# A window of three row transfers and two tiles on GpSimd's queue in place of bursts of four: a two-pass mixture-of-experts block with local attention

## The chip, the core and the metric

The kernel runs on one core of one Trainium2 chip. The metric is the device time of one execution in microseconds (us), as the median of several executions. Five engines work in parallel and wait for each other through semaphores: PE (matrix products), DVE (vector), ACT (activations), POOL (GpSimd) and SP (a queue that only issues transfers). Here POOL issues all indirect (scattering) transfers, and SP all others.

## The reference

The input is 32 sequences of 256 tokens with 128 channels. Half of a mixture-of-experts layer is added to it, then attention over the last 9 positions, then half of the same mixture-of-experts layer again:

```
x = x + 0.5 * ffn(layernorm(x))       # pass 1
x = x + attn(layernorm(x))
x = x + 0.5 * ffn(layernorm(x))       # pass 2

def ffn(xt):                          # 8192 tokens, 8 experts, 2 of them for each token
    probs, idx = top_k(softmax(xt @ Wg + bg), 2)
    h  = gelu(xt @ W1[e] + b1[e])     # 128 -> 512
    eo = h @ W2[e] + b2[e]            # 512 -> 128
    return probs[0] * eo[idx[0]] + probs[1] * eo[idx[1]]
```

Attention has 16 heads of 8 channels; each position sees itself and the 8 before it.

## The kernel before

The tokens lie in SBUF in 4 groups of 2048. Both passes go over the groups; the text counts the group scatters of both passes as q = 0 to 7 (q = 4 is group 0 in pass 2). For the experts the work is cut into seven parts: groups 0, 1, 2 and 3 of pass 1 are a part each (0 to 3), groups 0 and 1 of pass 2 are part 4 together, group 2 is part 5, group 3 is part 6.

For each group the router (DVE's `route`) works out a slot for each token and choice. ACT (`highs`) and DVE (`lows`) make the rows that are to be scattered, in four chunks of eight rows into the two halves of the buffer `hl`; a row is 128 tokens with 144 words each. POOL (`scatter_rows`, line 579) sends each row with one indirect transfer to the DRAM tensor `x_sorted` of its part, where it is sorted by expert. A chunk's half of `hl` is free for the chunk after next when all its rows have landed: ACT waits for that at line 669 before the cast at line 670. When all rows of a part have landed (`rows_sorted`, line 456) and the part's plan is ready, SP begins to load the part's tiles (`load_x`, lines 466 and 470): 256 or 128 slots of one expert, transposed, and their row numbers and gates, `tile_ids`.

PE multiplies a tile with W1 (line 949) and W2 (lines 960 and 966), with ACT's gelu between (line 756). DVE (`take_y`, line 1412) scales the result into `y_sb`, which has four places; it waits until the results of the tile four before have landed. POOL (`scatter_y`, line 596) scatters them to `y_pairs`, with two transfers for a wide tile of 256 slots and one for a narrow tile. SP loads the ids of a tile only when the results of the tile eight before have landed. When a part's results have all landed they are read back as `y_in` and added to x.

What each engine does in which order is fixed: five strings (`PE_ORDER`, `DVE_ORDER` and so on) say from which stream of work the engine issues its next step, and every engine issues strictly in that order. A step that waits holds up all that stands behind it on the same engine. On POOL the streams are the rows (`s`) and the tiles' results (`y`).

In pass 1 POOL issues a chunk's eight rows one after the other with no wait between. In pass 2 it issues four rows (`BURST`), then waits until all four have landed, before it takes its next step. Results of tiles are issued as soon as DVE has written them. `carry_waits` is one semaphore instruction, put ahead of a transfer to hold its waits.

Of the kernel before, what the change touches and what calls it, by code (L numbers as in the profile page):

```python
# [41 lines left out]
J = 16  # L42
# [9 lines left out]
Q = 4  # L52
JQ = J // Q
# [3 lines left out]
DMA = 16  # L57
SPLITS = (((0,), (1,), (2,), (3,)), ((0, 1), (2,), (3,)))
LOADS = 4
SUMMED_BY_DVE = (1, 3, 5, 7)  # L60
BURST = 4
B2_LO = 32
ROOT_START = 1597463007.0

# [95 lines left out]
def macaron(nc, x, Wq, Wk, Wv, Wo, Wg, bg, W1, b1, W2, b2, out):  # L160
    B, S, _ = x.shape
    N = B * S
    G = N // (P * J)
    PARTS = [gs for parts in SPLITS for gs in parts]
    PASS = [f for f, parts in enumerate(SPLITS) for _ in parts]
# [21 lines left out]
    def y_moves(ring, n):  # L187
        return DMA * sum(t.halves for t in ALL_TILES[:n] if t.ring == ring)
# [9 lines left out]
    with ExitStack() as ctx:  # L198
        def sb(name, shape, dt):
            return ctx.enter_context(nc.sbuf_tensor(name, shape, dt))  # L200

        def sem(name):
            return ctx.enter_context(nc.semaphore(name))

        def sems(name, n):
            return [sem(f"{name}{i}") for i in range(n)]
# [27 lines left out]
        hl = sb("hl", [P, 2, JQ, 2, ROW // 2], F32)  # L234
# [117 lines left out]
        hi_ready = sem("hi_ready")  # L352
        hl_ready = sem("hl_ready")
        slots_ready = sem("slots_ready")
        rows_scattered = sems("rows_scattered", 2)
        plan_ready = sem("plan_ready")
        ends_ready = sem("ends_ready")
        tails_cleared = sems("tails_cleared", NP)
# [23 lines left out]
        y_scattered = sems("y_scattered", 4)  # L382
# [5 lines left out]

        N_CONSTS = 9
        POOL_STEPS = 21 + NP  # L390
        SCATTERS = J * DMA

        def sums_before(g, c):

# [5 lines left out]
        def carry_waits(eng):  # L400
            eng.sem_inc(waits_carried)
# [29 lines left out]
        def _(sp):  # L431
# [24 lines left out]
            def rows_sorted(p):  # L456
                sp.wait_ge(tails_cleared[p], (1 + E) * DMA)
                sp.wait_ge(plan_ready, p + 1)
                for r in range(2):
                    sp.wait_ge(rows_scattered[r], (PASS[p] * G + PARTS[p][-1] + 1) * SCATTERS)  # L460

            def load_x(t):
                row = sp.value_load(tile_row[0:1, t.in_map:t.in_map + 1], min_val=0, max_val=SLOTS[t.p] - t.slots)
# [15 lines left out]
            def tiles():  # L479
                for t in ALL_TILES:  # L480
                    if t.at == 0:
                        clear_tails(t.p)
                        rows_sorted(t.p)
                    load_x(t)
                    yield
# [46 lines left out]
        def _(pool):  # L532
# [17 lines left out]
                               in_=window_mask[:].rearrange("p (j w) -> p j w", w=W), compare_op=ALU.is_ge,  # L550
# [3 lines left out]
                               in_=earlier[:].rearrange("o (e f) -> o e f", f=E), compare_op=ALU.is_gt,  # L554
# [16 lines left out]
            def scatter_rows(f, g):  # L571
                q, p = f * G + g, PART_OF[f * G + g]
                pool.wait_ge(slots_ready, q + 1)
                for c in range(Q):
                    pool.wait_ge(hl_ready, Q * q + c + 1)
                    carry_waits(pool)
                    for i in range(2 * JQ):
                        at = g * (J * 2) + c * (2 * JQ) + i
                        pool.indirect_dma_start(  # L579
                            out=x_sorted[p],  # L580
                            out_offset=bass.IndirectOffsetOnAxis(ap=slots_all[:, at:at + 1], axis=0),
                            in_=hl[:, c % 2, i // 2, i % 2, :], in_offset=None).then_inc(rows_scattered[c % 2], DMA)
                        if f and (i + 1) % BURST == 0:
                            pool.wait_ge(rows_scattered[c % 2], q * SCATTERS + (c // 2 * (2 * JQ) + i + 1) * DMA)
                            carry_waits(pool)
                            if i + 1 < 2 * JQ:
                                yield
                    yield

            def scatter_y():  # L590
                for t in ALL_TILES:
                    pool.wait_ge(ids_loaded[t.n % IDS], (t.n // IDS + 1) * DMA)
                    pool.wait_ge(y_ready, t.n + 1)
                    carry_waits(pool)
                    for i in range(t.halves):
                        pool.indirect_dma_start(  # L596
                            out=y_pairs, out_offset=bass.IndirectOffsetOnAxis(ap=tile_ids[:, t.n % IDS, i, 0:1].bitcast(U32), axis=0),
                            in_=y_sb[:, t.ring, i, :], in_offset=None, bounds_check=2 * N - 1, oob_is_err=False
                        ).then_inc(y_scattered[t.ring], DMA)
                    yield  # L600
# [10 lines left out]
        def _(act):  # L611
# [52 lines left out]
            def highs():  # L664
                for q in range(2 * G):
                    for c in range(Q):
                        act.wait_ge(norm_r.xn_ready, q * PAIRS + (c + 1) * (PAIRS // Q))
                        if q or c >= 2:
                            act.wait_ge(rows_scattered[c % 2], q * SCATTERS + c // 2 * (2 * JQ * DMA))
                        act.copy(hl16[:, c % 2, :, :, 0:D], xn_at[q][:, c * JQ:(c + 1) * JQ, :].rearrange("p j (o d) -> p j o d", o=1)  # L670
                                 .to_broadcast([P, JQ, 2, D])).then_inc(hi_ready, 1)
                        yield
# [769 lines left out]
```

## Time and profile before

| | |
|---|---|
| time of three executions | 1208.0, 1210.67 and 1205.4 us, median 1208.0 |
| span of the profiled execution, first to last instruction | 1193.9 us |
| PE busy | 919.0 us (77%) |
| POOL busy | 669.9 us (56%) |
| DVE busy | 644.4 us (54%) |
| ACT busy | 500.2 us (42%) |
| indirect transfers of rows | 256 |
| indirect transfers of results | 305 |

The profile is of one more execution, whose own time is not among the three; its span is 14.1 us below their median. "Busy" counts only execution, not waiting: an engine that is busy for less than the span waits for the rest, and what it waits for is read from the timelines and the chain below. In a timeline the brackets at the end of a row hold the idle time of the engine just before that instruction, and what ended it.

### The profile page before, as it was taken

How to read it: one execution, taken by the hardware profiler on the slowest of the kernel's cores; microseconds unless marked ns; L12 is line 12 of the kernel's file. 1: busy time of each engine (PE TensorE's matmuls, PEld its weight loads, DVE VectorE, ACT ScalarE, POOL GpSimd, SP SyncE). 2: the span in 40 equal slices, each digit the busy share in tenths (PEclk: the TensorE clock that was granted, in tenths of full speed). 3: DMA queues.
4: the chain of work that ended last, by engine and by line, in shares of the span. 5: the costliest groups of instructions: out<-in, count | busy, mean ns of one | idle time of the engine just before them, and what ended most of it. 6: DMA issues, size and time to landing. Idle time of an engine off the chain costs nothing.

```text
span 1193.9 us, 22506 instructions
## 1 busy us (share of the span) xinstructions
PE 919.0 (77%) x6345; PEld 762.5 (64%) x6345; DVE 644.4 (54%) x1309; ACT 500.2 (42%) x1215; POOL 669.9 (56%) x593
## 2 busy tenths in 40 slices
PE   3446868567897798988898838998988868865984
PEld 3334747456775587777777725677766756754874
DVE  6655133423147587898979998687851511110222
ACT  4433524334534273655644415634434433322432
POOL 2475445446387766455668556356765555555452
PEclk9999769889898799999999978989985988897997
DMA  8813212252113421026112121223222223432683
GB/s 274 235 55 73 55 44 50 65 137 67 42 58 62 134 54 41 19 59 139 33 39 55 23 96 55 45 52 68 50 60 53 51 59 84 116 97 69 154 190 120
DMA packets 170344, 96.44 MB, mean 81 GB/s; under 512 B 137696, under 2 KB 154390, under 8 KB 169332
## 3 DMA queue, kind: packets, MB, share of 16 engines
q1 hardware_dynamic: 152276, 59.29, 21.9%
q0 software_dynamic: 17952, 35.71, 9.5%
q8 instruction: 60, 0.98, 0.4%
q14 instruction: 56, 0.46, 0.1%
HBM read 25.77 MB, written 52.35 MB: 65 GB/s over the span
## 4 chain that ended last, share of the span: by engine, by line
PE 41%; issue 16%; DMA 10%; POOL 9%; another core or an unknown queue 8%; DVE 6%; SPq 6%; ACT 3%; ACTq 0%; POOLq 0%; DVEq 0%
PE bank L966 18%; PE bank L949 12%; POOL x_sorted L579 7%; DMA x_sorted<-hl,slots_all 5%; PE bank L854 3%; DMA x_sb<-in_L_attn_x 2%; PE bank L960 2%; ACT h_f L756 1%; POOL y_pairs L596 1%; SPq L476 1%; PE bank L840 1%; PE bank L867 1%; SPq L466 1%; SPq L452 1%
## 5 line engine op out<-in xcount | busy, mean ns | idle before, releaser
L596 POOL DMA_INDIRECT y_pairs<-y_sb,tile_ids x305 | 359.5, 1179 | 330.0 <-issue 215.9
L756 ACT ACTIVATE h_f<-bank,b_cols 128x256 f32<-128x256 f32 (+1 forms) x736 | 264.1, 439 | 443.3 <-PE bank L949 298.3
L579 POOL DMA_INDIRECT x_sorted<-hl,slots_all x256 | 301.9, 1179 | 179.4 <-issue 86.8
L966 PE MATMUL bank<-w_sb,h_f 128*128 x2440 | 355.2, 299 | 22.6 <-issue 15.3
L966 PEld LDWEIGHTS bank<-w_sb,h_f 128*128 128x128 f32 x2440 | 315.3, 206 | 45.1 <-issue 28.2
L949 PE MATMUL bank<-xsT,w_hl 128*128 128x256 f16 (+1 forms) x2208 | 263.3, 270 | 56.6 <-issue 20.9
L949 PEld LDWEIGHTS bank<-xsT,w_hl 128*128 x2208 | 201.2, 104 | 93.8 <-issue 66.7
L1412 DVE TENSOR_TENSOR y_sb<-bank,tile_ids 128x256 f32<-128x256 f32 (+1 forms) x184 | 68.8, 375 | 342.2 <-PE bank L966 169.0
L960 PE MATMUL bank<-b_hl,ones_b 64*128 x184 | 49.5, 269 | 72.8 <-DVE y_sb L1412 59.8
L960 PEld LDWEIGHTS bank<-b_hl,ones_b 64*128 64x128 f16 x184 | 17.1, 93 | 113.2 <-issue 110.6
L1197 DVE TENSOR_TENSOR prod<-score,qkv 128x2304 f32<-128x2304 f32 x32 | 81.6, 2550 | 0.2
L1151 DVE TENSOR_TENSOR prod<-qkv 128x2304 f32<-128x2304 f32 x32 | 81.4, 2551 | 0.2
L867 PE MATMUL bank<-prod,ident 128*128 128x256 f32 x288 | 67.3, 384 | 2.9 <-DVE prod L1197 2.5
L854 PE MATMUL bank<-prod,ident 128*128 128x288 f32 x256 | 65.4, 413 | 0.4 <-DVE prod L1151 0.4
L685 ACT COPY qkv<-bank 128x384 f32<-128x384 f32 (+1 forms) x96 | 41.3, 450 | 50.1 <-PE bank L840 22.2
L867 PEld LDWEIGHTS bank<-prod,ident 128*128 128x128 f32 x288 | 53.7, 192 | 10.7 <-DVE prod L1197 3.6
L854 PEld LDWEIGHTS bank<-prod,ident 128*128 128x128 f32 x256 | 49.1, 194 | 15.2 <-DVE prod L1151 1.5
L1035 DVE TENSOR_TENSOR hl<-xn_r,hl 128x1024 f16<-128x1024 f32 x24 | 29.3, 1223 | 43.3 <-ACT hl L670 33.9
L840 PE MATMUL bank<-wqkv,xnT_p 128*128 128x384 f32 x128 | 48.8, 509 | 3.5 <-ACT qkv L685 3.5
L670 ACT CAST hl<-xn_r 128x1024 f16<-128x1024 f32 x24 | 24.9, 1044 | 59.4 <-DMA x_sorted<-hl,slots_all 59.4
L614 ACT ACTIVATE xn_r<-x_sb,shift_r,rstd_r 128x128 f32<-128x128 f32 x96 | 39.0, 486 | 10.7 <-DVE shift_r L1022 10.7
L793 PE MATMUL bank<-wg_sb,xnT_p 128*128 128x8 f32 x128 | 27.8, 358 | 8.8 <-issue 5.6
(159 smaller groups left out, 851.3 us busy)
## 6 DMA issues: line engine op xcount, KB each, us to landing
y_in<-y_pairs SPq DMA_DIRECT2D x28, 512.0 KB
x_sorted<-no_rows SPq DMA_DIRECT2D x7, 720.0 KB
y_pairs<-y_sb,tile_ids POOLq DMA_INDIRECT x305
x_sb<-in_L_attn_x SPq DMA_DIRECT2D x4, 1024.0 KB, 5.7
x_sorted<-hl,slots_all POOLq DMA_INDIRECT x256
x_sorted<-no_rows SPq DMA_DIRECT2D x56, 72.0 KB
out<-x_sb SPq DMA_DIRECT2D x3, 1024.0 KB
xsT<-x_sorted SPq DMA_TRANSPOSE x184
```

The source lines that it names most:

```text
L579: pool.indirect_dma_start(out=x_sorted[p], out_offset=bass.IndirectOffsetOnAxis(ap=slots_all[:, at:at + 1], axis=0), in_=hl[:, c % 2, i // ...
L596: pool.indirect_dma_start(out=y_pairs, out_offset=bass.IndirectOffsetOnAxis(ap=tile_ids[:, t.n % IDS, i, 0:1].bitcast(U32), axis=0), in_=y ...
L756: ins = act.activation(h_part(t, b)[:, k, :], bank[h_banks.uses[u][0]][:, k * t.slots:(k + 1) * t.slots], ACT.Gelu, bias=b1_cols[:, bass.d ...
L840: pe.matmul(prep_bank[k % PREPS][:, 0:3 * D], xnT_p[:, k - RADIUS, 1:1 + P], wqkv[:], start=True, stop=True).then_inc(qkv_done, 1)
L854: ins = pe.matmul(score_bank[c % 2][:, 0:JH * W * HEADS].rearrange("p (n h) -> p n h", h=HEADS), ident[:], products[:, :, d, :], start=(d ...
L867: ins = pe.matmul(score_bank[c % 2][:, 0:JH * D].rearrange("p (j d) -> p j d", d=D), ident[:], prod[:, c % 2, :, w, :], start=(w == 0), st ...
L949: ins = pe.matmul(dst, w1_flat[:, bass.ds((e * HC + c) * (2 * P) + ws * P, P)], slots_of(t)[:, s], start=(n == 0), stop=(n == 2))
L960: pe.matmul(into, ones_b2[:], b2_hl[:, bass.ds(e * D, D)].rearrange("k (o d) -> k o d", o=1) .to_broadcast([2 * B2_LO, t.halves, D]), star ...
L966: ins = pe.matmul(into[:, half, :], h_part(t, c // t.per)[:, c % t.per, half * P:(half + 1) * P], w2_flat[:, bass.ds((e * HC + c) * D, D)] ...
L1151: ins = dve.tensor_tensor(prod[:, prod_of[c]], q_ap.to_broadcast([P, JH, W, D]), windows(lo, D), ALU.mult)
L1197: dve.tensor_tensor(prod[:, c % 2].rearrange("p j w (h d) -> p j w h d", d=DK), score[:, lo:lo + JH].rearrange("p j w (h o) -> p j w h o", ...
L1412: dve.tensor_tensor(y_sb[:, t.ring, 0:t.halves], y_bank(t), tile_ids[:, t.n % IDS, 0:t.halves, 1:2] .to_broadcast([P, t.halves, D]), ALU.m ...
```

## The change

The bursts of four are dropped. Rows are counted through both passes (`n`), and from the fourth on each waits, before it is issued, until the row three before it has landed; the semaphores of rows are four (`n % 4`) in place of two (one for each half of `hl`). So at most three rows are in flight, in both passes. Results of a tile wait until the results of the tile two before have landed. ACT and SP wait for the same rows as before, on four semaphores in place of one or two.

```
-BURST = 4
+WINDOW = 3
+ROW_RING = 4
...
-        rows_scattered = sems("rows_scattered", 2)
+        rows_scattered = sems("rows_scattered", ROW_RING)
...
-        SCATTERS = J * DMA
+        CHUNK = 2 * JQ // ROW_RING * DMA
...
-                for r in range(2):
-                    sp.wait_ge(rows_scattered[r], (PASS[p] * G + PARTS[p][-1] + 1) * SCATTERS)
+                for r in range(ROW_RING):
+                    sp.wait_ge(rows_scattered[r], (PASS[p] * G + PARTS[p][-1] + 1) * Q * CHUNK)
...
                     pool.wait_ge(hl_ready, Q * q + c + 1)
-                    carry_waits(pool)
                     for i in range(2 * JQ):
                         at = g * (J * 2) + c * (2 * JQ) + i
+                        n = (q * Q + c) * (2 * JQ) + i
+                        if n >= WINDOW:
+                            pool.wait_ge(rows_scattered[(n - WINDOW) % ROW_RING], ((n - WINDOW) // ROW_RING + 1) * DMA)
+                        carry_waits(pool)
                         pool.indirect_dma_start(
                             out=x_sorted[p],
                             out_offset=bass.IndirectOffsetOnAxis(ap=slots_all[:, at:at + 1], axis=0),
-                            in_=hl[:, c % 2, i // 2, i % 2, :], in_offset=None).then_inc(rows_scattered[c % 2], DMA)
-                        if f and (i + 1) % BURST == 0:
-                            pool.wait_ge(rows_scattered[c % 2], q * SCATTERS + (c // 2 * (2 * JQ) + i + 1) * DMA)
-                            carry_waits(pool)
-                            if i + 1 < 2 * JQ:
-                                yield
+                            in_=hl[:, c % 2, i // 2, i % 2, :], in_offset=None).then_inc(rows_scattered[n % ROW_RING], DMA)
+                        if f and i + 1 == JQ:
+                            yield
                     yield
...
                     pool.wait_ge(y_ready, t.n + 1)
+                    if t.n >= 2:
+                        pool.wait_ge(y_scattered[(t.n - 2) % 4], y_moves((t.n - 2) % 4, t.n - 1))
                     carry_waits(pool)
...
                         if q or c >= 2:
-                            act.wait_ge(rows_scattered[c % 2], q * SCATTERS + c // 2 * (2 * JQ * DMA))
+                            for r in range(ROW_RING):
+                                act.wait_ge(rows_scattered[r], (q * Q + c - 1) * CHUNK)
```

The order of the instructions stays the same on every engine; only waits differ. On POOL, at the start of pass 1, the first rows of part 0 stand so before (`x_sorted0` is that part's tensor, "x7" seven alike in a row):

```order
L579 DMA x_sorted0<-hl,slots_all 18688x144 [waits hl_ready,pool_step,slots_ready]
L579 DMA x_sorted0<-hl,slots_all 18688x144 x7
L579 DMA x_sorted0<-hl,slots_all 18688x144 [waits hl_ready]
L579 DMA x_sorted0<-hl,slots_all 18688x144 x7
L579 DMA x_sorted0<-hl,slots_all 18688x144 [waits hl_ready]
```

And so with the change (`rows_scattered0` to 3 are the four semaphores in turn):

```order
L583 DMA x_sorted0<-hl,slots_all 18688x144 [waits hl_ready,pool_step,slots_ready]
L583 DMA x_sorted0<-hl,slots_all 18688x144 x2
L583 DMA x_sorted0<-hl,slots_all 18688x144 [waits rows_scattered0]
L583 DMA x_sorted0<-hl,slots_all 18688x144 [waits rows_scattered1]
L583 DMA x_sorted0<-hl,slots_all 18688x144 [waits rows_scattered2]
L583 DMA x_sorted0<-hl,slots_all 18688x144 [waits rows_scattered3]
L583 DMA x_sorted0<-hl,slots_all 18688x144 [waits rows_scattered0]
L583 DMA x_sorted0<-hl,slots_all 18688x144 [waits hl_ready,rows_scattered1]
```

No row but the chunk's first had a wait; now every row from the fourth on waits for the one three before it.

On POOL, the end of part 5's results and the last rows of part 6 (`x_sorted6`; `ids_loaded` and `y_ready` belong to the results) stand so before:

```order
L596 DMA y_pairs<-y_sb,tile_ids 16384x128 [waits ids_loaded0,y_ready]
L596 DMA y_pairs<-y_sb,tile_ids 16384x128 [waits ids_loaded1,y_ready]
L579 DMA x_sorted6<-hl,slots_all 18688x144 x4
L579 DMA x_sorted6<-hl,slots_all 18688x144 [waits rows_scattered0,hl_ready]
L579 DMA x_sorted6<-hl,slots_all 18688x144 x3
L579 DMA x_sorted6<-hl,slots_all 18688x144 [waits rows_scattered1]
L579 DMA x_sorted6<-hl,slots_all 18688x144 x3
L596 DMA y_pairs<-y_sb,tile_ids 16384x128 [waits rows_scattered1,ids_loaded2,y_ready]
```

And so with the change:

```order
L599 DMA y_pairs<-y_sb,tile_ids 16384x128 [waits y_scattered2,ids_loaded0,y_ready]
L599 DMA y_pairs<-y_sb,tile_ids 16384x128 [waits y_scattered3,ids_loaded1,y_ready]
L583 DMA x_sorted6<-hl,slots_all 18688x144 [waits rows_scattered1]
L583 DMA x_sorted6<-hl,slots_all 18688x144 [waits rows_scattered2]
L583 DMA x_sorted6<-hl,slots_all 18688x144 [waits rows_scattered3]
L583 DMA x_sorted6<-hl,slots_all 18688x144 [waits rows_scattered0]
L583 DMA x_sorted6<-hl,slots_all 18688x144 [waits hl_ready,rows_scattered1]
L583 DMA x_sorted6<-hl,slots_all 18688x144 [waits rows_scattered2]
```

The waits between the bursts have become waits of each row for the third before it. The results behind the rows no longer wait for those rows (`rows_scattered1` in the last line of before), but, as the first two lines here, for the results of the tile two before.

## Rows read from the trace of the kernel before

**Rows 1.** The page's chain that ended last, by engine and line.
```profile
PE 41%; issue 16%; DMA 10%; POOL 9%; another core or an unknown queue 8%; DVE 6%; SPq 6%; ACT 3%; ACTq 0%; POOLq 0%; DVEq 0%
PE bank L966 18%; PE bank L949 12%; POOL x_sorted L579 7%; DMA x_sorted<-hl,slots_all 5%; PE bank L854 3%; DMA x_sb<-in_L_attn_x 2%; PE bank L960 2%; ACT h_f L756 1%; POOL y_pairs L596 1%; SPq L476 1%; PE bank L840 1%; PE bank L867 1%; SPq L466 1%; SPq L452 1%
```

**Rows 2.** Waits of POOL: who waited for whom, total us, times, longest.
```profile
POOL x_sorted L579 <- DMA x_sorted<-hl,slots_all: 48.4, 21, 4.1
...
POOL y_pairs L596 <- DMA x_sorted<-hl,slots_all: 15.9, 6, 3.5
```

**Rows 3.** POOL's timeline in pass 2: start, us, instruction, [idle before <-releaser].
```profile
620.18 0.99 POOL L596 DMA_INDIRECT y_pairs<-y_sb,tile_ids  x1 [2.49 <-DMA x_sorted<-hl,slots_all]
...
857.16 1.97 POOL L596 DMA_INDIRECT y_pairs<-y_sb,tile_ids  x1 [2.33 <-DMA x_sorted<-hl,slots_all]
...
1006.12 0.99 POOL L596 DMA_INDIRECT y_pairs<-y_sb,tile_ids  x1 [4.54 <-DVE y_sb L1412]
...
1059.23 0.99 POOL L596 DMA_INDIRECT y_pairs<-y_sb,tile_ids  x1 [3.51 <-DMA x_sorted<-hl,slots_all]
...
1077.04 0.95 POOL L579 DMA_INDIRECT x_sorted<-hl,slots_all  x1 [0.30 <-issue]
1080.22 0.96 POOL L579 DMA_INDIRECT x_sorted<-hl,slots_all  x1 [2.23 <-DMA x_sorted<-hl,slots_all]
...
1087.12 0.96 POOL L579 DMA_INDIRECT x_sorted<-hl,slots_all  x1 [2.15 <-DMA x_sorted<-hl,slots_all]
...
1094.17 0.99 POOL L596 DMA_INDIRECT y_pairs<-y_sb,tile_ids  x1 [2.31 <-DMA x_sorted<-hl,slots_all]
```

**Rows 4.** The chain in order of time, two stretches: start, us, what.
```profile
693.98 4.29 DMA x_sorted<-hl,slots_all
...
1077.04 2.29 DMA x_sorted<-hl,slots_all
1079.37 0.08 issue
1079.46 0.76 issue
```

**Rows 5.** POOL's timeline in pass 1, where rows and results alternate.
```profile
346.19 1.00 POOL L596 DMA_INDIRECT y_pairs<-y_sb,tile_ids  x1 [0.30 <-issue]
347.50 0.96 POOL L579 DMA_INDIRECT x_sorted<-hl,slots_all  x1 [0.30 <-issue]
```

**Rows 6.** POOL's timeline at the seventh row of all.
```profile
50.02 4.94 POOL L579 DMA_INDIRECT x_sorted<-hl,slots_all  x1 [0.30 <-issue]
```

**Rows 7.** POOL's transfers, 46 to 48 us: packets, MB, share of 16 engines.
```profile
q0 software_dynamic: 27, 0.05, 8.7%
```

**Rows 8.** DVE's timeline at seven places.
```profile
49.70 4.41 DVE L1292 SCALAR_TENSOR_TENSOR w_hl<-qkv,w_hl 128x4096 f16<-128x4096 f32 x1
...
623.87 0.42 DVE L1412 TENSOR_TENSOR y_sb<-bank,tile_ids 128x256 f32<-128x256 f32 x1 [4.31 <-issue]
...
725.10 1.22 DVE L1035 TENSOR_TENSOR hl<-xn_r,hl 128x1024 f16<-128x1024 f32 x1 [2.99 <-ACT hl L670]
...
743.96 0.19 DVE L1356 TENSOR_TENSOR tile_expert<-onehot 1x40 int32<-1x40 f32 x1
...
877.47 1.23 DVE L1035 TENSOR_TENSOR hl<-xn_r,hl 128x1024 f16<-128x1024 f32 x1 [2.93 <-ACT hl L670]
...
1011.86 0.42 DVE L1412 TENSOR_TENSOR y_sb<-bank,tile_ids 128x256 f32<-128x256 f32 x1 [1.64 <-remote]
...
1096.71 0.29 DVE L1412 TENSOR_TENSOR y_sb<-bank,tile_ids 128x128 f32<-128x128 f32 x1 [10.40 <-DMA y_pairs<-y_sb,tile_ids]
```

**Rows 9.** PE's timeline at the ends of the scatters of q = 4 and 5.
```profile
619.61 4.15 PE L854 MATMUL bank<-prod,ident 128*128 128x288 f32 x16 [0.39 <-DVE prod L1151]
...
762.45 1.93 PE L949 MATMUL bank<-xsT,w_hl 128*128 128x256 f16 x12 [2.75 <-DMA xsT<-x_sorted]
```

**Rows 10.** ACT's timeline at the last cast of q = 5.
```profile
724.02 1.04 ACT L670 CAST hl<-xn_r 128x1024 f16<-128x1024 f32 x1 [4.45 <-DMA x_sorted<-hl,slots_all]
```

## The prediction, made before the changed kernel ran

> **What bounds the kernel now.** I began with the chain of work that ended last. No engine fills it: PE holds 41%, and 5% are landings of rows (`DMA x_sorted<-hl,slots_all`) beside 7% of POOL issuing them [rows 1]. Landings stand on a chain only where somebody stands still until a transfer is down, so next I read POOL's waits: 27 waits on rows, 48.4 + 15.9 = 64.3 us in all [rows 2]. In pass 1 POOL has no such wait in the code; these are the drains behind the bursts of pass 2. POOL's timeline shows how one looks: after the fourth row of a burst the engine idles 2.23 us where it idles 0.30 us between two rows [rows 3]. The chain splits that wait: the row lands 2.29 us after its issue began, and POOL starts again 0.08 + 0.76 = 0.84 us later [rows 4]. Whether a drain costs the kernel anything must be read at each place, from what DVE, ACT and PE do at that moment: their orders are fixed, and work that reaches them earlier is of use only if they are idle waiting for it.
>
> **What the window itself costs.** Between rows POOL needs 0.96 + 0.30 = 1.26 us [rows 3], so the row three before began 3.78 us earlier. It has landed after 2.29 us and could release its waiter at 2.29 + 0.84 = 3.13 us [rows 4]. That leaves 0.65 us, and in undisturbed stretches the window never binds: in pass 1 it is then no change at all, and in pass 2 only the drains go. The same sum holds for two wide tiles of results (four transfers, the last of tile t-2 beginning some 3.9 us ahead of tile t). Two narrow tiles back to back would lose 3.13 - 2.6 = 0.5 us a pair, but PE brings them more slowly than POOL issues them. The added semaphore instruction ahead of each row I price at nothing: where rows and results alternate in pass 1, each with such an instruction ahead, the gap stays 0.30 us and a step takes 1.26 to 1.30 us [rows 5]. Were the 0.04 us above 1.26 its price, part 0's 32 rows would lose 1.3 us. ACT's and SP's two or three further waits are on semaphores long reached; the 0.08 us piece after a landing bounds what one adds [rows 4].
>
> **Where the window does bind: the first rows.** Up to about 50 us SP's loads and clears fill the DMA engines, and POOL's transfers moved 0.05 MB in 2 us, less than one row of 128 x 576 bytes [rows 7]. Before, six rows were issued into that; the seventh then hung on GpSimd for 4.94 us beside DVE's 4.41 us weight split, which began 0.3 us before it [rows 6, 8]. With the window only four or so are out before that split, so about two are pushed behind it: 2 x 1.26 = 2.5 us later for part 0, and PE's first tile waits for its last row. Bounds: 0 (the wait lies inside the split) and 5 us (four rows). I take +2.5.
>
> **What the lost drains give, place by place.** A drain that goes saves its idle time less 0.30.
>
> *End of q = 4's scatter (620 us).* Some 15 us go from POOL, eight drains like the 2.49 us one [rows 3]. But here DVE is all but fully busy with attention; only its `take_y` at 623.87 waits 4.31 us [rows 8], and the next things wait for PE's 16 products, which run to 619.61 + 4.15 = 623.76 anyway [rows 9]. Gain about 0.5; bounds 0 and 4.3.
>
> *q = 5 (690 to 762 us).* POOL would save about 15 us again. The last part of the chunk casts on ACT waits 4.45 us for landings [rows 10], and DVE behind it 2.99 us [rows 8]. With the rows landing some 7 us earlier both waits go; DVE then gains 2.99. At the end PE waits 2.75 us for part 4's first tile [rows 9]. The rows will be down well before, and the plan, ready at 743.96 + 0.19 [rows 8], is no limit either. What stands behind is attention on PE, so no more than 2.99 + 2.75 = 5.7 comes out of 15. Bounds 2.8 and 8.
>
> *q = 6 (812 to 900 us).* A drain of 2.33 us stands in POOL's unbroken run of results and rows [rows 3], whose end releases ACT's cast, for which DVE waits 2.93 us [rows 8]. Gain 2.33 - 0.30 = 2.0; bounds 0 and 2.9.
>
> *Part 5's first results (1006 us).* POOL idles 4.54 us ahead of them [rows 3]; the reason shown is DVE, but the burst just before is still landing. DVE's next `take_y`, four tiles on, waits 1.64 us [rows 8]. Gain 1.6; bounds 0 and 4.2.
>
> *Part 5 to part 6 (1055 to 1097 us).* Nothing else is left here: attention is over, and DVE stands 10.40 us until the results issued at 1094.17 land [rows 3, 8]; PE stands with it. Those results wait in POOL's order behind twelve rows, and part 6's tiles wait for the same rows. Four drains lie on that one line: 3.51, 2.23, 2.15 and 2.31 us [rows 3], less 4 x 0.30 = 9.0 us. Lower bound 5.1, if the first (ahead of results that may wait for PE) is hidden and SP's clearing of tails holds the last 0.7.
>
> **Sum.** -0.5 - 5.7 - 2.0 - 1.6 - 9.0 = -18.8, and +2.5, makes -16.3 us. The profiled span of 1193.9 becomes 1177.6. What lies outside the span, 14.1 us against the median, I leave as it is: 1208.0 - 16.3 = 1191.7, so 1192. The bounds put together, not all at one end, are about 1180 and 1205.
>
> **The rivals.**
>
> *Every drain was on the path.* For it speaks that the chain has 5% of landings [rows 1], nearly as much as all drains. Then 64.3 - 27 x 0.30 = 56 us go, less 2.5: 1154 us. Against it: DVE's and PE's rows at q = 4 show that 15 us there buy half of one.
>
> *The fixed orders take it all back.* What POOL saves at q = 5 and 6 may only lengthen the next wait of DVE for PE. If nothing but the last place stays, with its lower bound 5.1 and the start's +2.5, the kernel gains 2.6 us: 1205. For it: five of the seven DVE rows shown wait for something [rows 8], and behind each stands another engine.
>
> *Landings are slower than 3 us where it counts (slower).* One drain's row landed only after 4.29 us, while y_in was loaded [rows 4]. If rows mostly landed like that, a row would wait 4.29 + 0.84 - 3.78 = 1.35 us in every three, 0.45 us a row. Four rows then lose 1.8 us to the window where a drain cost 1.9, so pass 2 gains nothing, and part 0's 32 rows lose 14.4 us ahead of PE's first tile: 1208 + 2.5 + 14.4 = 1225. With landing time L the gain of 18.8 shrinks by (L - 2.94) / 3 / 0.475 of itself, and part 0 loses 32 (L - 2.94) / 3; the two and the 2.5 balance at L = 3.6 us, from which on the kernel is slower. Against it: all but a few of the drains shown are near 2.2 us, and the share of the DMA engines is high only at the two ends of the span. The Trainium skill's page "DMA: Bandwidth & Descriptors" ("Latency and other measured facts") speaks for this rival: it gives HBM access as 0.2 us on average and 2 us under high load, and calls it the main part of a transfer's fixed cost. By that rule a landing beside heavy loads would take 2.29 + 1.8 = 4.1 us (an estimate from that page), and were all of part 0's rows so loaded the time would be near 1222; the 4.29 us row agrees with it, the 2.29 us rows show that it is the exception.
>
> **How the numbers follow.** Chances: forecast 0.66, all drains 0.07, given back 0.16, slow landings 0.11. The forecast gives 1192, its own range 1180 to 1205. To leave out no more than 2 in 10 the range takes in the given-back case and something below and above: 1172 to 1211. A measurement of this kernel can tell about 0.5%, 6 us, from no change. Faster than 1202: nine tenths of the forecast's case and all drains, 0.67. Within 6 us: the rest of the forecast's and most of the given-back case, 0.21. Slower: 0.12.
>
> **What would show it.** In the profile of the changed kernel POOL's waits on rows fall from 64 us to under 15, most of them before 60 us. The gap between rows stays 0.30 us in pass 1 from 60 us on. The first tile's load comes 2 to 3 us later. Between the end of part 5 and the start of part 6 DVE's wait of 10.40 us shrinks by 6 to 9 us, and PE's wait for part 4's first tile is gone. I am wrong if rows in quiet stretches wait for each other (landings or the added instruction cost more than I read), if results queue behind the two-tile wait so that DVE's `take_y` waits grow, or if the engines' waits only move.

## The result, and the profile after

The changed kernel is slower: 1242.6 us, median of four executions (1236.3 to 1251.3), against 1209.3 us for the kernel before beside it (1205.4 to 1211.7). The ratio is 1.031, with a 95% interval of 1.026 to 1.035. The prediction, 1192 us with a range of 1172 to 1211, has the wrong sign. The profiled execution spans 1236.4 us, 42.5 us more than before. In all that follows, an execution more than 1.5% above the fastest of its kernel is left out of the ratios.

The page of the changed kernel, busy line and chain (to be held against [rows 1]):

```profile
PE 926.0 (75%) x6345; PEld 766.6 (62%) x6345; DVE 643.9 (52%) x1309; ACT 500.8 (41%) x1215; POOL 660.5 (53%) x593
...
PE 44%; DVE 16%; another core or an unknown queue 13%; issue 12%; ACT 5%; DMA 3%; SPq 3%; POOL 2%; ACTq 0%; DVEq 0%; POOLq 0%
```

POOL is on the chain (the work that ended last) with 2% where it had 9, and landings of all kinds with 3% where they had 10: the drains are gone from it, as intended. But 13% is now "another core or an unknown queue", where it was 8. POOL's waits in the changed kernel (who waited for whom, total us, times, longest) say the same as [rows 2] and what was foretold:

```profile
POOL y_pairs L599 <- DVE y_sb L1416: 103.7, 24, 40.0
...
POOL y_pairs L599 <- DMA y_pairs<-y_sb,tile_ids: 36.6, 22, 3.9
POOL x_sorted L583 <- DMA x_sorted<-hl,slots_all: 22.5, 48, 3.1
```

Waiting for rows has fallen from 64.3 to 22.5 us; the two-tile wait is new and small. The 40.0 us is a wait for DVE. POOL's timeline in the changed kernel (start, us, instruction, idle before and its end):

```profile
49.10 0.96 POOL L583 DMA_INDIRECT x_sorted<-hl,slots_all  x1 [3.15 <-DMA x_sorted<-hl,slots_all]
51.02 3.94 POOL L583 DMA_INDIRECT x_sorted<-hl,slots_all  x1 [0.97 <-DMA x_sorted<-hl,slots_all]
...
88.97 0.95 POOL L583 DMA_INDIRECT x_sorted<-hl,slots_all  x1 [0.31 <-issue]
107.51 0.96 POOL L583 DMA_INDIRECT x_sorted<-hl,slots_all  x1 [17.59 <-DVE hl L1050]
...
755.21 0.96 POOL L583 DMA_INDIRECT x_sorted<-hl,slots_all  x1 [0.30 <-issue]
796.14 2.47 POOL L599 DMA_INDIRECT y_pairs<-y_sb,tile_ids  x1 [39.96 <-DVE y_sb L1416]
...
1126.31 0.96 POOL L583 DMA_INDIRECT x_sorted<-hl,slots_all  x1 [0.30 <-issue]
1127.57 0.99 POOL L599 DMA_INDIRECT y_pairs<-y_sb,tile_ids  x1 [0.30 <-issue]
```

The same four places in the kernel before (the last row of part 0, the first of part 1, the last row of q = 5, part 4's first result):

```profile
87.75 0.96 POOL L579 DMA_INDIRECT x_sorted<-hl,slots_all  x1 [0.30 <-issue]
95.83 0.96 POOL L579 DMA_INDIRECT x_sorted<-hl,slots_all  x1 [7.12 <-issue]
...
756.62 0.96 POOL L579 DMA_INDIRECT x_sorted<-hl,slots_all  x1 [0.30 <-issue]
772.80 2.47 POOL L596 DMA_INDIRECT y_pairs<-y_sb,tile_ids  x1 [15.22 <-DVE y_sb L1412]
```

So part 0 ends only 1.2 us later, yet part 1 begins 11.7 us later. The rows of q = 5 are even down 1.4 us earlier than before, and still part 4's first result comes 23.3 us later. Time is lost after POOL has done its work, on another engine. Which one, the timelines of PE, DVE and ACT in the changed kernel show at these two places:

```profile
78.04 1.14 PE L827 MATMUL bank<-chosen,ones 128*128 128x128 bf16 x16
...
93.84 0.29 DVE L1097 TENSOR_TENSOR xnT_r<-bank,region 128x128 f32<-128x128 f32 x1 [19.85 <-remote]
...
746.16 1.60 PE L841 MATMUL bank<-wqkv,xnT_p 128*128 128x256 f32 x4
756.12 1.22 PE L841 MATMUL bank<-wqkv,xnT_p 128*128 128x256 f32 x2 [8.36 <-issue]
...
755.70 0.37 ACT L689 COPY qkv<-bank 128x256 f32<-128x256 f32 x1 [10.62 <-remote]
```

DVE's step at line 1097 waits for one thing of another engine, PE's products of lines 825 and 827. By the trace they are over at 78.04 + 1.14 = 79.2; DVE gets them at 93.84, 14.6 us later. "remote" is what the profile prints when a semaphore rises and no recorded instruction ends then. The Trainium skill, page "Perfetto Trace Analysis", section "Summary: the profiler window per engine type", says that TensorE's end in a profile is an estimate; the trace agrees, and here the estimate is 14.6 us early. At 746 us it is the same: four products of line 841, then no more for 8.36 us, and ACT gets one of them at 755.70. Both times POOL issues rows 1.27 us apart meanwhile, the last at 88.97 and 755.21, and the products come through within 5 us of that. In the kernel before the same step of DVE got the same products 4.0 us after their recorded end:

```profile
75.12 1.14 PE L823 MATMUL bank<-chosen,ones 128*128 128x128 bf16 x16
...
80.21 0.29 DVE L1093 TENSOR_TENSOR xnT_r<-bank,region 128x128 f32<-128x128 f32 x1 [9.22 <-remote]
```

Rows went out 1.26 us apart there too, but two of them, at 69.95 and 71.97, stood 2.02 us apart; with the window they follow each other at 1.27 us from 63.67 to the end of part 0.

What the drains had done shows best between the results of part 5 and those of part 6, where POOL issues twelve rows. In the kernel before DVE takes three results meanwhile, the first and the last of them while POOL stands in the drains that end at 1080.22 and 1087.12 [rows 3]:

```profile
1079.36 0.29 DVE L1412 TENSOR_TENSOR y_sb<-bank,tile_ids 128x128 f32<-128x128 f32 x1 [5.78 <-remote]
...
1086.02 0.29 DVE L1412 TENSOR_TENSOR y_sb<-bank,tile_ids 128x128 f32<-128x128 f32 x1 [4.38 <-PE bank L966]
```

In the changed kernel the rows go out from 1112.39 on without a gap, and after its step at 1113.10 DVE takes none until they are over:

```profile
1113.10 0.29 DVE L1416 TENSOR_TENSOR y_sb<-bank,tile_ids 128x128 f32<-128x128 f32 x1 [2.84 <-issue]
1131.09 0.29 DVE L1416 TENSOR_TENSOR y_sb<-bank,tile_ids 128x128 f32<-128x128 f32 x1 [17.70 <-remote]
```

Such waits are what has grown most. The waits of ACT and DVE put down to "remote", in the kernel before and in the changed one:

```profile
ACT h_f L756 <- remote: 131.3, 28, 12.3
DVE y_sb L1412 <- remote: 131.0, 24, 15.4
```

```profile
ACT h_f L760 <- remote: 155.8, 30, 16.8
DVE y_sb L1416 <- remote: 136.2, 21, 17.7
DVE xnT_r L1097 <- remote: 37.1, 4, 19.9
DVE x_sb L1247 <- remote: 33.6, 3, 17.5
```

Over all rows of that view ACT waits 142.8 and DVE 154.6 us before, 187.6 and 206.9 after: each some 45 to 52 us more, about what the span has grown by (42.5). Below, "late products" is the sum of the two: 297 us before, 394 after.

### The profile page after: what moved, and what is told of

Same layout as the page of the kernel before. It is cut to its first block, busy times and chain, and to the rows that moved or that the text cites. A ratio compares the mean times of both kernels' runs of the same rounds, so it can differ in the third digit from the quotient of the medians.

```text
span 1236.4 us, 22924 instructions
## 1 busy us (share of the span) xinstructions
PE 926.0 (75%) x6345; PEld 766.6 (62%) x6345; DVE 643.9 (52%) x1309; ACT 500.8 (41%) x1215; POOL 660.5 (53%) x593
## 4 chain that ended last, share of the span: by engine, by line
PE 44%; DVE 16%; another core or an unknown queue 13%; issue 12%; ACT 5%; DMA 3%; SPq 3%; POOL 2%; ACTq 0%; DVEq 0%; POOLq 0%
PE bank L970 17%; PE bank L953 11%; PE bank L858 3%; PE bank L871 2%; PE bank L844 2%; DVE prod L1201 2%; DVE prod L1155 2%; PE bank L964 2%; DMA x_sorted<-hl,slots_all 2%; PE bank L841 2%; ACT h_f L760 2%; DVE prod L1166 2%; DVE y_sb L1416 1%; PE bank L797 1%
## 5 line engine op out<-in xcount | busy, mean ns | idle before, releaser
L599 POOL DMA_INDIRECT y_pairs<-y_sb,tile_ids x305 | 357.3, 1172 | 386.2 <-issue 245.9
L583 POOL DMA_INDIRECT x_sorted<-hl,slots_all x256 | 294.5, 1151 | 175.0 <-DVE hl L1050 77.0
L970 PE MATMUL bank<-w_sb,h_f 128*128 x2440 | 361.0, 301 | 24.2 <-issue 18.7
L970 PEld LDWEIGHTS bank<-w_sb,h_f 128*128 128x128 f32 x2440 | 319.7, 208 | 49.0 <-issue 31.9
L871 PE MATMUL bank<-prod,ident 128*128 128x256 f32 x288 | 70.4, 396 | 4.6 <-DVE prod L1201 4.5
```

The source lines that it names most:

```text
L583: pool.indirect_dma_start(out=x_sorted[p], out_offset=bass.IndirectOffsetOnAxis(ap=slots_all[:, at:at + 1], axis=0), in_=hl[:, c % 2, i // ...
L599: pool.indirect_dma_start(out=y_pairs, out_offset=bass.IndirectOffsetOnAxis(ap=tile_ids[:, t.n % IDS, i, 0:1].bitcast(U32), axis=0), in_=y ...
L871: ins = pe.matmul(score_bank[c % 2][:, 0:JH * D].rearrange("p (j d) -> p j d", d=D), ident[:], prod[:, c % 2, :, w, :], start=(w == 0), st ...
L970: ins = pe.matmul(into[:, half, :], h_part(t, c // t.per)[:, c % t.per, half * P:(half + 1) * P], w2_flat[:, bass.ds((e * HC + c) * D, D)] ...
```

## The experiments

Theory A: while GpSimd issues transfers back to back, TensorE's products stop coming through, and the drains, by their silences, had let them through. Rivals: B, the two-tile wait holds up results; C, the window on rows costs; D, what counts in a drain is the limit on transfers in flight; E, rows that come earlier than the fixed orders expect do harm. Ratios are to the kernel before, run beside; its median lay between 1195.8 and 1209.3 us from one comparison to the next.

**Which part of the change does it.** `no_y_wait` is the change without its two-tile wait:

```
-                    if t.n >= 2:
-                        pool.wait_ge(y_scattered[(t.n - 2) % 4], y_moves((t.n - 2) % 4, t.n - 1))
```

> The change without its two-tile wait of results; the window of three rows stays in both passes. Theory A (pauses): where GpSimd issues transfers back to back, matrix products that the trace has as begun report to ACT and DVE only about 3 us after GpSimd falls silent; the drains of before broke the rows of pass 2 every four, the change does not. Then the two-tile wait is not the cause, and as it makes some pauses among results itself, this kernel is as slow as the change or slower: 1235 to 1265 us. Rival B (the two-tile wait holds up results): this kernel falls to about 1190 to 1210 us. Rival C (the window on rows costs): it stays at 1230 to 1245.

Measured: 1226.2 us, ratio 1.027 (1.019 to 1.034); the kernel before took 1195.8 us here, 1.1% less than the expectations start from. `y_wait_only` puts these two lines, and nothing else, into the kernel before:

> The kernel before, with its bursts of four, and the two-tile wait of results added. A: 1190 to 1212 us, no slower than before, since the drains are still there and the wait adds pauses. B: 1225 to 1245 us. C: 1208.

Measured: 1195.9 us, ratio 1.000 (0.996 to 1.004). B is out. `no_drain` is the kernel before with the drains taken out:

```
-                        if f and (i + 1) % BURST == 0:
-                            pool.wait_ge(rows_scattered[c % 2], q * SCATTERS + (c // 2 * (2 * JQ) + i + 1) * DMA)
-                            carry_waits(pool)
-                            if i + 1 < 2 * JQ:
-                                yield
+                        if f and i + 1 == JQ:
+                            yield
```

> The kernel before without its drains in pass 2, and with neither window nor two-tile wait. A: the drains were what let the matrix products through, so 1225 to 1260 us, as slow as the change. B and C, and the prediction made before the run, say that drains only cost: 1180 to 1200 us.

Measured: 1221.3 us, ratio 1.018 (1.011 to 1.026), with 348 us of late products. Doing away with the drains alone makes the kernel slower; they were worth more than they cost. `no_y_wait` is `no_drain` with the window of three. Measured side by side it is 0.4% slower and their times overlap (1222.4 to 1232.4 against 1212.9 to 1226.4 us), so C is at most a small part. `burst_both` adds drains to pass 1:

```
-                        if f and (i + 1) % BURST == 0:
+                        if (i + 1) % BURST == 0:
...
-                            if i + 1 < 2 * JQ:
+                            if f and i + 1 < 2 * JQ:
```

> The kernel before with the drain behind every four rows in pass 1 too (32 more drains of some 1.9 us each on GpSimd's queue). A: the long waits of ACT and DVE for products in pass 1 (166 us together between 40 and 551 us in the kernel before) shrink by half or more, and the kernel gets faster: 1150 to 1200 us. B and C: drains cost GpSimd time and give nothing, 1208 to 1235 us.

Measured: 1197.5 us, ratio 0.999 (0.995 to 1.003). A's gain did not come. Late products between 40 and 555 us sum to 167 us, where it was 166. Results are still issued unbroken there; `paced_rows` below shows what they do.

**Silence, order, or a limit in flight.** `pause4` is `no_drain` with four writes of GpSimd into a small tensor of its own behind every four rows of pass 2; `late_rows` has the same writes, 32 of them, ahead of each group's first row:

```
+                        if f and (i + 1) % JQ == 0:
+                            pause(pool, 4)
```

```
                 pool.wait_ge(slots_ready, q + 1)
+                if f:
+                    pause(pool, 32)
```

> The kernel before without its drains, with a pause in their place: after every four rows of pass 2 GpSimd writes four times into a small tensor of its own (about 2 us) and waits for no transfer. Theory A (silence of GpSimd is what lets matrix products through): as fast as before, a ratio of 0.99 to 1.01. Rival D (the drain matters because it limits the rows in flight or makes later transfers wait for earlier ones): as slow as without drains, 1.015 to 1.03.

> The same pauses in sum, but all ahead of a group's first row in pass 2 (32 writes, some 16 us), and then its 32 rows with no drain. Rival E (rows that come earlier than the fixed orders were made for do the harm, not the lack of silences): ratio 0.99 to 1.01. A: the rows are as unbroken as without drains, and the 16 us come on top where rows are waited for: 1.02 to 1.05.

Measured: `pause4` 1210.5 us, ratio 1.005 (1.001 to 1.010); `late_rows` 1258.6 us in the one execution that counts for a ratio, 1.043 of before, and 1279.8 to 1284.2 in the three others. Pauses that wait for no transfer give back most of what the drains gave, so D is out; rows that are late but unbroken are slower, by what A expected, so E is out. Against A stands that late products are 420 us in `pause4`. Some of that is no effect of the edit: in pass 1, whose code is the same in all of them, they sum to 166 us before, 172 in `no_drain` and 220 in `pause4`, so the sum is a rough measure. In pass 2 they are 131, 176 and 199 us; none of the waits of `pause4` there is longer than 11.5 us, where `no_drain` has 17.6, but the sum did not fall. `break_all` is `burst_both` with the results of a tile waiting for those of the tile just before:

```
+                    if t.n >= 1:
+                        pool.wait_ge(y_scattered[(t.n - 1) % 4], y_moves((t.n - 1) % 4, t.n))
```

> The kernel before with the drain behind four rows in both passes, and results of a tile waiting until those of the tile before it have landed, so that GpSimd never issues more than four transfers without a silence. A: no product is reported more than some 8 us late anywhere, and the waits of ACT and DVE for such products fall by a third or more (297 us in the kernel before); against it stand GpSimd's added waits, so a ratio of 0.96 to 1.00. The two-tile rival B: 1.02 to 1.06.

Measured: 1398.3 us, ratio 1.160 (1.152 to 1.167). Late products fell to 53 us, by far more than a third, but at that price: landings are 39% of its chain. A was right on the products and wrong on the time.

**The disputed cost by itself.** In `micro` TensorE only repeats a group of 12 f16 and 16 f32 products, ACT copies each group out, and GpSimd scatters rows that nobody waits for. The trace records each f32 product as two, so a group counts as 44 below. `micro`, `micro2` and `micro3` ran once each; what is compared are stretches of one execution. Four stretches differ in how the rows go out:

```
if what == "window" and n >= 3:
    pool.wait_ge(landed[(n - 3) % 4], ((n - 3) // 4 + 1) * DMA)
pool.indirect_dma_start(out=dest, out_offset=..., in_=rows[:], in_offset=None).then_inc(landed[n % 4], DMA)
...
if what == "spaced":
    pool.memset(idle[:], 0.0)
```

> The disputed cost by itself: everything of the kernel is left out (the output is a copy of x), TensorE runs 110 equal groups of 28 products and ACT copies each group out; GpSimd scatters 40 rows four times over, and nothing of TensorE waits for it: back to back (from group 15), in drained bursts of four (from 40), with the window of three (from 65), with a pause of its own of some 0.5 us behind each row (from 90). A: a group takes the same 3 to 8 us as without rows in the drained stretch and the spaced one, and in the back-to-back and window stretches ACT gets no group for tens of us, until GpSimd falls silent. If GpSimd's transfers do not hold TensorE up, all stretches show the same time per group; then A is wrong in its mechanism and the silences do something else.

The windows view (start and end, length, then busy us and instructions of PE, PEld, ACT and POOL, granted clock, share of the DMA engines, GB/s) of a stretch without rows, back to back, without rows, bursts of four, window of three, spaced:

```profile
80.00:100.00 20.00, 20.00 (x183) 19.46 (x182) 1.92 (x4) 0.00 (x0) 1.00 0.00 1
112.00:150.00 38.00, 9.89 (x29) 6.99 (x28) 0.48 (x1) 28.86 (x31) 0.54 0.16 58
160.00:180.00 20.00, 20.00 (x169) 19.50 (x168) 1.44 (x3) 0.00 (x0) 0.92 0.00 1
270.00:336.00 66.00, 66.00 (x597) 64.23 (x597) 6.23 (x13) 35.74 (x38) 1.00 0.12 43
400.00:440.00 40.00, 10.65 (x37) 7.39 (x35) 0.48 (x1) 30.01 (x32) 0.57 0.16 57
560.00:620.00 60.00, 60.00 (x543) 58.36 (x542) 5.75 (x12) 54.03 (x73) 1.00 0.13 46
```

Products per us: 183 / 20 = 9.2 alone, 29 / 38 = 0.8 back to back, 37 / 40 = 0.9 with the window of three, and 9.0 both in drained bursts (1.75 us from row to row in the mean) and spaced (1.67). ACT's timeline at the start of the back-to-back stretch, whose rows go out from 101.7 to 152.2 us:

```profile
105.27 0.48 ACT L73 COPY back<-bank 128x384 f32<-128x384 f32 x1 [4.40 <-PE bank L64]
127.38 0.48 ACT L73 COPY back<-bank 128x384 f32<-128x384 f32 x1 [21.63 <-remote]
158.45 0.48 ACT L73 COPY back<-bank 128x384 f32<-128x384 f32 x1 [30.60 <-remote]
```

A group that takes 4.88 us alone takes 22.1, then 31.1, and ACT's wait has the same name as in the kernel, "remote". Nothing of TensorE waits for GpSimd here, so cause and effect are not in doubt. The group at 127.38 arrives in the midst of the rows: the products slow down to a tenth of their pace; they do not stop, which is what A had said. `micro2` asks how much of a pause is needed; its pairs are (every how many rows, how many words):

```
-WHAT = ("free", "burst", "window", "spaced")
+WHAT = ("free", "signal", (1, 1), (1, 128), (1, 256), (2, 512), (4, 512))
```

> Again TensorE's equal groups alone beside 32 rows of GpSimd seven times over (the output is a copy of x): back to back; with a semaphore instruction behind each row; with one write of 1, 128 or 256 words a partition behind each row; with a write of 512 words (0.54 us) behind every second and every fourth row. Theory A as the first such run showed it: some work of GpSimd other than a transfer, in between, lets the products through. If its length counts, the 1-word write helps little and the 512-word write behind every second row nearly as much as behind every one; if any other instruction of GpSimd is enough, already 1 word does. The semaphore instruction changes nothing (the change has one ahead of each row): a group takes over 20 us there, against 4.9 us without rows.

Its windows, in the order of the expectation (back to back, semaphore, 1, 128 and 256 words behind each row, 512 behind every second, behind every fourth):

```profile
76.00:112.00 36.00, 17.08 (x113) 14.87 (x112) 0.96 (x2) 27.26 (x29) 0.68 0.16 56
208.00:244.00 36.00, 15.46 (x99) 11.40 (x96) 0.50 (x2) 27.16 (x29) 0.65 0.16 58
341.00:377.00 36.00, 15.93 (x104) 12.22 (x102) 0.72 (x2) 30.12 (x57) 0.70 0.16 56
474.00:513.00 39.00, 24.80 (x142) 19.07 (x140) 1.16 (x3) 33.55 (x57) 0.69 0.15 54
605.00:646.00 41.00, 35.04 (x245) 29.50 (x243) 2.39 (x5) 36.36 (x57) 0.92 0.15 51
722.00:763.00 41.00, 35.53 (x276) 30.57 (x273) 2.39 (x5) 34.40 (x42) 1.00 0.14 50
834.00:872.00 38.00, 25.25 (x147) 20.66 (x145) 0.96 (x2) 30.42 (x35) 0.67 0.15 53
```

Each window begins with 8 us or more at full speed. Products per us are 3.1, 2.8, 2.9, 3.6, 6.0, 6.7 and 3.9. From one row's start to the next (first to last start, by their count) these stretches took 1.27, 1.26, 1.26, 1.36, 1.46, 1.46 and 1.35 us: it is the mean pace that counts, not the kind of instruction in between, nor its place. A had expected 512 words behind every second row to be worth nearly as much as behind every row; they give 6.7 products per us, where `micro` had 9.0 with the write behind every row. `micro3` varies what a transfer carries:

```
wide, parts = 8 if what == "narrow" else ROW, 16 if what == "few" else P
```

> TensorE's equal groups alone a third time (the output is a copy of x), beside 32 transfers of GpSimd back to back of four kinds: whole rows (128 x 144 words, scattered); the same scattered rows cut to 8 words; rows of 144 words from 16 partitions only; and plain transfers of 128 x 144 words without indices. If it is GpSimd's issuing that holds the products up, all kinds that it issues as close together do it, whatever they carry; if it is the amount that the DMA engines move, the cut rows and those of 16 partitions leave a group at 4.9 us.

Its windows: whole rows, 8 words, 16 partitions, plain transfers:

```profile
76.00:112.00 36.00, 18.04 (x120) 15.46 (x117) 0.96 (x2) 27.04 (x28) 0.69 0.16 56
208.00:244.00 36.00, 17.19 (x109) 13.16 (x106) 0.69 (x2) 26.98 (x29) 0.71 0.03 4
341.00:373.00 32.00, 12.45 (x86) 10.11 (x84) 0.48 (x1) 23.47 (x28) 0.68 0.04 8
475.00:492.00 17.00, 17.00 (x155) 16.50 (x154) 1.71 (x4) 16.43 (x31) 1.00 0.36 127
```

Transfers that move 4 or 8 GB/s in place of 56 hold the products up just the same (3.3, 3.0 and 2.7 per us), so bytes are not it. Plain transfers, 0.53 us apart and at 127 GB/s, do nothing (9.1); their stretch is only 17 us long, but in its last 7 us TensorE still did 65 products, where beside whole rows it did 16 in the 7 us that begin as late. So it goes with GpSimd's indirect transfers, not with every transfer of GpSimd.

**Back in the kernel.** `paced_change` is the change, `paced_all` is `no_drain`, and `paced_rows` is `no_drain` with rows alone paced, each with one write of 512 words:

```
                             in_=hl[:, c % 2, i // 2, i % 2, :], in_offset=None).then_inc(...)
+                        pause(pool)
...
                         ).then_inc(y_scattered[t.ring], DMA)
+                        pause(pool)
```

> The change with one write of 512 words a partition into a tensor of GpSimd's own (0.54 us, 0.40 us more from one transfer to the next) behind every row and every single transfer of results; window and two-tile wait stay. Theory A (transfers closer together than some 1.6 us hold TensorE's products up): although GpSimd has 561 x 0.40 = 224 us more to do, the late reports of products (remote waits of ACT and DVE, 394 us in the change) fall by half or more, and the time falls below the change's 1.031 of before: a ratio of 0.96 to 1.01. If the loss of the change were anything else, more work for GpSimd could only make it slower: 1.03 to 1.10.

> The same writes in the kernel before without its drains and with neither window nor two-tile wait. A: 0.96 to 1.01, equal to the paced change within 1%, since with the pace kept the windows cost and give nothing. Otherwise above 1.02, slower than without drains.

> The write behind rows alone, in both passes; results are issued back to back as before. A: 0.97 to 1.01; faster than all transfers paced if the runs of results are too short to hold TensorE up for long (some eight transfers pass in the run alone before a product is late), slower if not.

Measured: `paced_change` 1193.2 us, ratio 0.999 (0.996 to 1.002); `paced_all` 1177.4, 0.988 (0.980 to 0.995); `paced_rows` 1188.2, 0.997 (0.992 to 1.001). Late products fall to 15 us in the first, 12 in the second, and only to 281 in the third: it was the runs of results that made most of them, and that no drain had ever broken. In time it is the other way round: from 1.018 without drains to 0.997 with the rows paced, and to 0.988 with the results paced too. With 224 us more work on GpSimd the change loses its whole 3.1%. `paced_all` is bound by that work (POOL has 54% of its chain); `paced_384` and `paced_256` shorten the write:

```
-        idle = sb("idle", [P, 512], F32)
+        idle = sb("idle", [P, 384], F32)
```

> The paced kernel (a write behind every row and every transfer of results, no drains, no windows) with 384 words a partition in place of 512, which leaves some 1.56 us from one transfer to the next in place of 1.67. TensorE alone ran free at 1.67 and at half its speed at 1.46. If the loss sets in at a pace between the two, the late reports of products are still few here, GpSimd (54% of the chain in the paced kernel) saves 561 x 0.1 = 56 us of its own, and the time falls: a ratio of 0.96 to 0.985. If 1.56 is already too close, the late reports come back and the ratio is 0.985 to 1.01.

> The same with 256 words, 1.46 us from one transfer to the next, at which a group of TensorE alone took 8 to 9 us in place of 4.9: the late reports of ACT and DVE are back in the hundreds of us, and the time is that of the kernel before or worse, 0.99 to 1.02.

Measured: `paced_384` 1163.5 us, ratio 0.962 (0.957 to 0.967), the only version that beats before by more than 2%; `paced_256` 1192.1, 0.987 (0.983 to 0.992), a little better than expected. The busy line and chain of `paced_384`, and its largest late products:

```profile
PE 898.4 (77%) x6345; PEld 748.8 (64%) x6345; DVE 656.1 (56%) x1309; ACT 501.2 (43%) x1215; POOL 909.7 (78%) x1154
...
POOL 27%; PE 26%; issue 10%; DVE 8%; another core or an unknown queue 7%; SPq 6%; DMA 4%; ACT 2%; POOLq 0%; DVEq 0%; ACTq 0%
```

```profile
DVE y_sb L1421 <- remote: 123.2, 27, 7.9
ACT h_f L765 <- remote: 76.5, 25, 6.2
```

POOL and PE now hold the chain about equally. Late products are 210 us at this pace, 328 with 256 words and 12 with 512: the loss sets in gradually, between 1.67 and 1.46 us from one transfer to the next, and of the three lengths the middle one, with POOL at 27% of the chain in place of 54%, is the fastest. That the time does not follow the sum alone shows in `paced_256`, faster than before with more late products (328 against 297 us).

## Why the prediction was wrong, point by point

- **The failed step** is the one that prices a drain: "A drain that goes saves its idle time less 0.30." For POOL that held; for the kernel a drain was not only a cost: results came through inside two of the drains named (1079.36 and 1086.02 above). `no_drain` does exactly this step and is 1.8% slower, where the five drain terms promised 18.8 us less.
- **"The fixed orders" and the place-by-place terms.** At q = 5 POOL saved more than the 15 us named: its first row is 18.1 us late against before, its last 1.4 us early. The gain of 5.7 became a loss: part 4 was to begin with its rows down, since "the plan, ready at 743.96 + 0.19 [rows 8], is no limit either". The plan now ends at 771.5 us, 27 us later than before: the group began 18 us late, and attention's products on PE were held up beside those very rows (755.70, above). At part 5 to part 6 POOL did save what was foretold: from the first of the twelve rows to the result behind them it takes 15.2 us where it took 20.9, and three of the four drains were priced at 5.8. But the kernel did not get the 9.0 us: DVE's wait there is 17.70 us "remote" where it was 10.40 [rows 8], and it ends at 1131.09, 2.5 us after the last of 14 transfers without a gap. The terms of q = 6 and part 5's first results are not seen at all: the rows of q = 6 go from 23.0 us late at the first to 35.4 at the last.
- **The window costs nothing in quiet stretches**: right. Rows wait 22.5 us in all, 4.1 of it in the two waits of the start shown above; the other 46 come to 0.4 us each, little more than the usual gap of 0.30. But "in pass 1 it is then no change at all" fails by its consequence: the start moved by a little, and part 1 then began 11.7 us late, through a late product of PE (93.84). That comes with the window: `no_y_wait` has it at 93.44, while `no_drain`, without the window, gets it at 80.27 and the kernel before at 80.21. By the first row of pass 2 the change is 9.2 us behind, `no_y_wait` 2.5 and `no_drain` 3.9; as `no_drain` has the pass 1 of before, some 4 us of that is the spread between profiles.
- **The start** was predicted at 2.5 us (0 to 5) and measured at 1.2, by the mechanism given: fewer rows out before DVE's weight split, the fifth taking 3.94 us beside it.
- **The two-tile wait** was rightly priced at nothing: 36.6 us on POOL, ratio 1.000 by itself. With the pace kept it is not quite free: `paced_change` took 1193.2 us beside 1177.4 of `paced_all`, 1.3% more, window and wait together, where at most 1% was expected.
- **The rivals.** Slow landings, the one on the slower side, did not happen; the time it named, 1225 us, was closer than the forecast's by accident. Its other figure, near 1222, leaves pass 2 no gain at all; by its own formula a landing of 4.1 us leaves 3.6 us, which makes 1219. No rival held the true cause. The trace had it: "another core or an unknown queue" stood at 8% of the chain [rows 1], and 262 us of "remote" waits in two lines were never followed up.
- **What stays open.** `no_drain` loses 1.8% (to 2.6) and the change 3.1% (from 2.6): the rest comes with the window and the two-tile wait together; `no_y_wait` puts 0.4% of it on the window, within the noise. Why `pause4` is nearly as fast as before with no fewer late products is not settled either. The spans and clocks of all these executions are the profiler's, so whether the loss is as large without its recording was not tested.

## What to carry to other kernels

A wait on one engine can be what lets another work, so before a stall is removed, look at what the other engines finish during it. When a profile shows waits on semaphores that rise with no recorded end beside them, follow those first: here they told that TensorE was later than its recorded work says. Where GpSimd issues many indirect transfers beside TensorE, a short piece of work behind each, here 0.45 us, was worth more than drains, windows or no waits at all.

## What the runs showed of the hardware that was not expected

TensorE did 0.8 to 0.9 products per us in place of 9.2 while GpSimd issued indirect transfers 1.27 us apart, after some 10 us of that pace, and ran free at 1.67 us; the amount carried made no difference, and plain transfers from the same queue did not do it. The granted clock fell too, to a mean of 0.54 in the held-up stretch, so mostly to the lower of its two levels (1.2 GHz), but after TensorE had begun to stand: from 111 to 115 us it did 11 products in 4 us, where it does 37 alone, at a granted clock still of 1.00. Nor does half the clock make a tenth of the products. The Trainium skill, page "Trainium Architecture — The Big Picture", section "What this means for kernel authors", has only VectorE and GpSimd contending for a port of SBUF, and engines and DMA never. By that alone a group beside GpSimd's rows would stay at 4.88 us; it took 22.1 and 31.1, so either the two contend for something other than these ports, or the measurement differs from the page. Which resource they share, no run here shows.
